# Two layers in one program: the second layer's first attentions beside the first layer's drain

## The reference

```python
x = x + tanh(g_xattn[0]) * L0_xattn(layernorm(x), ctx)   # 16 heads of 64, causal, key mask
x = x + tanh(g_ffn[0])   * L0_ffn(layernorm(x))          # attention between the 16 heads of a token,
                                                         # then 8 experts, summed by a softmax gate
x = x + tanh(g_xattn[1]) * L1_xattn(layernorm(x), ctx)   # 16 heads of 16, no mask
x = x + tanh(g_ffn[1])   * L1_ffn(layernorm(x))          # 2 experts of 256-1024-256 by top-1 of a token,
                                                         # and a shared one of the same size
```

## Time and profile before

| what | us |
|---|---|
| median of 3 runs | 2659.93 |
| the profiled execution | 2663.2 |
| its span | 2661.4 |
| one iteration of the first layer's loop | 78.4 |
| one iteration of the second layer's loop | 77.3 |
| first layer's two drain bodies | 65.0 and 32.0 |
| loads, splits and first projections of the second layer | 18.0 |
| second layer's body(0, None, 1) | 69.5 |

### The profile page before, as it was taken

How to read it: one execution, slowest core, us unless ns; L and a number is a source line. 1 busy time by engine, 2 the same in 40 slices (tenths; PEclk the granted TensorE clock), 3 DMA queues, 4 the chain that set the end, 5 groups by cost and what they waited for, 6 DMA issues and landing times. The chain is left out here.

```text
span 2661.4 us, 48220 instructions
## 1 busy us (share of the span) xinstructions
PE 2325.5 (87%) x16128; PEld 1931.7 (73%) x16128; DVE 1487.3 (56%) x3906; ACT 1268.0 (48%) x3971; POOL 1019.5 (38%) x910
## 2 busy tenths in 40 slices
PE   5888989888888898888466999999999999999998
PEld 4667777777777777776354777877777887777777
DVE  3467667666766676767635445444444544444441
ACT  5655566555556555556023444433344443334441
POOL 1355554555554455555512333222233322223320
PEclk9989999999999999999667999999999999999999
DMA  4000000000000000000040000000000000000000
GB/s 145 14 6 17 13 16 4 16 16 16 16 12 4 16 16 16 16 4 9 4 161 1 13 17 16 16 16 16 4 12 16 16 16 16 16 4 12 16 9 9
DMA packets 25856, 51.66 MB, mean 19 GB/s; under 512 B 6272, under 2 KB 7040, under 8 KB 24640
## 3 DMA queue, kind: packets, MB, share of 16 engines
q1 hardware_dynamic: 25792, 50.84, 5.7%
HBM read 42.44 MB, written 8.39 MB: 19 GB/s over the span
## 5 line engine op out<-in xcount | busy, mean ns | idle before, releaser
L1191 POOL TENSOR_SCALAR l_probs<-l_probs,l_rinv 128x256 f32<-128x256 f32 x512 | 238.4, 480 | 590.0 <-DVE l_rinv L1406 589.4
L1302 ACT ACTIVATE l_probs<-l_score,l_negmax 128x256 f32<-128x256 f32 x512 | 238.4, 472 | 265.0 <-DVE l_negmax L1401 265.0
L364 POOL TENSOR_TENSOR l_prod<-l_att,l_kv 128x2048 f32<-128x2048 f32 x64 | 287.4, 4527 | 180.7 <-DVE l_att L637 180.7
L350 POOL TENSOR_TENSOR l_prod<-l_q,l_kv 128x2048 f32<-128x2048 f32 x64 | 290.3, 4547 | 155.9 <-DVE l_att L620 84.1
L1606 PE MATMUL l_ffn<-l_w,l_hid 128*128 128x256 f32 x1536 | 347.9, 382 | 1.0 <-ACT l_hid L1276 1.0
L1606 PEld LDWEIGHTS l_ffn<-l_w,l_hid 128*128 128x128 f32 x1536 | 287.6, 190 | 51.0 <-issue 14.3
L1413 DVE COPY l_probsT<-l_attn 128x512 f32<-128x512 f32 x256 | 175.5, 685 | 161.1 <-PE l_attn L1569 160.9
L710 DVE CUSTOM_DVE_ANT_0 l_probs<-l_score,l_mbias 128x256 f32<-128x256 f32 (+1 forms) x512 | 161.3, 353 | 147.5 <-PE l_score L906 97.6
L1401 DVE TENSOR_REDUCE l_negmax<-l_score 128x2 f32<-128x512 f32 x256 | 175.1, 684 | 65.4 <-PE l_score L1557 65.4
L643 DVE TENSOR_REDUCE l_h<-l_prod 128x128 f32<-128x2048 f32 x64 | 146.3, 2286 | 110.7 <-POOL l_prod L364 110.7
L439 ACT ACTIVATE l_probs<-l_probs,l_negmax 128x256 f32<-128x256 f32 x256 | 130.8, 511 | 107.7 <-DVE l_negmax L710 106.5
(11 more groups left out here) (271 smaller groups left out, 7527.2 us busy)
## 6 DMA issues: line engine op xcount, KB each, us to landing
l_ctxin<-in_ctx SPq DMA_DIRECT2D x32, 256.0 KB, 3.0
l_xin<-in_x SPq DMA_DIRECT2D x16, 256.0 KB, 2.7
l_x<-in_x SPq DMA_DIRECT2D x16, 256.0 KB, 2.6
x<-l_acc SPq DMA_DIRECT2D x16, 256.0 KB, 2.0
l_xin<-x SPq DMA_DIRECT2D x16, 256.0 KB, 3.3
l_x<-x SPq DMA_DIRECT2D x16, 256.0 KB, 2.6
out<-l_x SPq DMA_DIRECT2D x16, 256.0 KB, 2.0
l_hid<-in_w SPq DMA_DIRECT2D x2, 1536.0 KB, 8.6
```

What stands on the lines that cost most here:

```text
L350: nc.gpsimd.tensor_tensor(prod[:, u].rearrange("p (h g d) -> p h g d", h=half, g=H), q4[:, u * half:(u + 1) * half].unsqueeze(2).to_broadc ...
L364: nc.gpsimd.tensor_tensor(prod[:, u].rearrange("p (h d g) -> p h d g", h=half, d=HD), a4.unsqueeze(2).to_broadcast([P, half, HD, H]), v4.u ...
L1191: last = nc.gpsimd.tensor_scalar(probs[:, j % 4, t * S:(t + 1) * S], probs[:, j % 4, t * S:(t + 1) * S], rinv[:, j, t:t + 1], 1.0, ALU.mul ...
L1302: last = nc.scalar.activation(probs[:, s % 4, t * S:(t + 1) * S], ps[:, t * S:(t + 1) * S], ACT.Exp, bias=negmax[:, s, t:t + 1], accum_out ...
```

## The change

`network` (new) builds both layers in one block. `layer0` and `layer1` no longer run a block; they return their five programs, now generators, and `side_by_side` interleaves the two programs of each engine by the position that each `yield` names. Both still have one order on each engine.

```diff
+BEGIN, BEGIN_OUT, TAIL = -0.8, -0.4, STEPS + 1
+FFN_LATE = STEPS - 6
+def side_by_side(*programs):
+    ahead = [(next(p), n, p) for n, p in enumerate(programs)]
+    while ahead:
+        _, n, p = ahead.pop(ahead.index(min(ahead)))
+        at = next(p, None)
+        if at is not None:
+            ahead.append((at, n, p))
```

Position 0 is step 0 of the first layer's last body with attention, `body(15, 14, 13)`; 21 (`TAIL`) is step 0 of the first drain body, 42 that of the second, whose steps are set half as far apart. The tail of every engine's program in layer0:

```diff
-                body(B - 1, B - 2, B - 3, None)
-                body(None, B - 1, B - 2, None)
-                body(None, None, B - 1, None)
+        for s in body(B - 1, B - 2, B - 3, None):
+            yield s
+        for s in body(None, B - 1, B - 2, None):
+            yield TAIL + s
+        for s in body(None, None, B - 1, None):
+            yield 2 * TAIL + s / 2
```

POOL's products of the mixing stand at 5.5, 6.5, 8.5, 9.5 and 13.5 to 16.5 of their body, the normalisation of head j of the second layer at j + 1. In layer1 the setup moves to the positions of body(15, 14, 13), body(0, None, 1) to those of the first drain body and body(1, 0, 2) to those of the second:

```diff
+    def sync(sp):
...
+        yield 6
+        _, full, _, turn = past.attn.at("q3", B - 1)
+        sp.wait_ge(full, turn)
+        load(0)
+        for n in range(NS_FIRST):
...
+        load(1)
+        yield TAIL + BEGIN
+        sp.wait_ge(past.x1_ready, B)
+        load_residual(0)
+        sp.dma_start(flat(wo), ins["wo1"]).then_inc(wo_in, 16)
+        for dst, src in late:
+            sp.dma_start(dst, src).then_inc(late_in, 16)
+        yield TAIL + STEPS
+        load(2)
+        yield 3 * TAIL
+        sp.wait_ge(past.x2_stored, 16 * B)
+        for n in range(NS_FIRST, NS):
+            sp.dma_start(raw(n), splits[n][0]).then_inc(raw_in[n % 2], 16)
+        sp.dma_start(flat(w2), ins["w2"]).then_inc(w2_in, 16)
+        load_residual(1)
+        store(0)
...
+    def scalar(act):
+        for n in range(NS_FIRST):
+            yield 9 + 2 * n
+            split(n)
+        yield TAIL + BEGIN
+        act.wait_ge(bias_ready, 1)
+        for use in attn.ahead:
+            project(use, 0)
+        for s in body(0, None, 1):
+            yield TAIL + s
+        for s in body(1, 0, 2):
+            yield 2 * TAIL + s
...
+    def vector(dve):
+        yield 9
+        pre_variance(0)
+        yield 11
+        split(0)
+        pre_normalise(0)
+        yield 13
+        split(1)
+        yield 15
+        split(2)
...
+        yield TAIL + BEGIN
+        dve.wait_ge(past.x1_ready, B)
+        for banks in (attn, score, heads):
+            banks.open(dve)
```

```diff
+    def up_at(b, s):
+        if first(b):
+            return range(12) if s == STEPS else ()
+        return (s,) if s < 12 else ()
```

On DVE, in step 12 and 13 of body(1, 0, None, 2), and on PE, behind the steps:

```diff
+                if first(b) and s == FFN_LATE - 2:
+                    dve.wait_ge(past.x2_ready, B)
+                    ffn.open(dve)
+                if first(b) and s == FFN_LATE - 1:
+                    for n in range(NS_FIRST, NS):
+                        split(n)
+                    begin(b)
...
+            if a is not None:
+                attn_out(a)
+            if b is not None:
+                if first(b):
+                    pe.wait_ge(split_lo, NS)
+                    for j in up_at(b, STEPS):
+                        ffn_up(b, j)
+                    pe.wait_ge(w2_in, 16)
+                    for piece in range(4):
+                        ffn_down(b, 0, piece)
+                for piece in range(4):
+                    ffn_down(b, 1, piece)
```

More of the change, by code:

```diff
@@ L8 @@
+from collections import namedtuple
 from contextlib import ExitStack
@@ L249, in layer0, with network @@
+def network(nc, ins, x2, out):
+    with ExitStack() as both:
+        with ExitStack() as left, ExitStack() as right:
+            one, past = layer0(nc, ins, x2, left, right, both)
+        with ExitStack() as left, ExitStack() as right:
+            two = layer1(nc, ins, x2, out, left, right, both, past)
         with nc.Block() as block:
@@ L289, in _ @@
-                load(2)
-                load_residual(1)
-                with sp.Fori(3, B) as b:
-                    load(b)
-                    load_residual(b - 1)
-                    store(b - 3)
-                load_residual(B - 1)
-                for b in (B - 3, B - 2, B - 1):
-                    store(b)
-                sp.wait_ge(x2_stored, 16 * B)
+                side_by_side(one.sync(sp), two.sync(sp))
             @block.gpsimd
             def _(pool):
-                nc.gpsimd.memset(ident[:], 0.0)
@@ L544, in _ @@
             def _(dve):
-                for banks in (attn, score, heads, side):
-                    banks.open(dve)
-                V = nc.vector
-                def variance(src, stat, mv, var, ready):
-                    for t in range(NT):
-                        V.bn_stats(stat[:, t], src[:, t])
-                    dve.drain()
-                    for t in range(NT):
-                        V.bn_aggr(mv[:, t], stat[:, t])
-                    dve.drain()
-                    V.tensor_scalar(var[:], mv[:, :, 1], LN_EPS, None, ALU.add).then_inc(ready, 1)
@@ L824, in _ @@
-                body(B - 1, B - 2, B - 3, None)
-                body(None, B - 1, B - 2, None)
-                body(None, None, B - 1, None)
+                side_by_side(one.vector(dve), two.vector(dve))
             @block.tensor
             def _(pe):
-                T = nc.tensor
-                def transpose4(banks, use, batch, src):
-                    ps, full, free, turn = banks.at(use, batch)
-                    pe.wait_ge(free, turn)
-                    for c in range(ND):
-                        for t in range(NT):
-                            last = T.transpose(ps[:, c * S + t * P:c * S + (t + 1) * P], src[:, t, c * P:(c + 1) * P], ident[:])
-                    last.then_inc(full, 1)
@@ L1683, in chunked @@
+                side_by_side(one.tensor(pe), two.tensor(pe))
 def chunked(w):
```

2626 lines of the change are left out of this document (1348 added, 1278 removed).

## The result

The changed kernel takes **2640.77 us** (median of 4 runs, 2637.36 to 2641.29), the kernel before beside it 2658.88: ratio 0.993, 95% interval 0.9913 to 0.9947. It is faster, and inside my range, but by 18 us where I had said 40. The profiled execution took 2640.78 us, its span 2639.0; the one of before took 2663.2, so the two profiles differ by 22.4 us, 4 more than the medians.

What follows compares the result with a forecast made beforehand. PE bounds the steady loop, but not the 269.1 us between the layers, forecast at 3.5 + 101 + 124.5 = 229. So 2663.2 - 40 = 2623, lowered by 3.3: 2620 us; own range 2608 to 2632, 8 in 10 2592 to 2648.

Steps and rivals of the forecast that it cites:

- (1): Second layer's setup moved under the first layer's last body: 3.5 us of delay there, 18 us between the layers gone.
- X: Mark where x1 of batch 15 is done, ending the first layer's last mixing body; forecast 3.5 us later, between 0 and 6.
- Wrong, if: Failure signs: A under 92 or over 112, w1 split waiting over 5 us for its transfer, later bodies not 77.3.
- (2): Second layer's attention of batch 0 beside the first layer's drain: 104 us, less 3 for the clock, 101.
- stage A: Stretch from x1 of batch 15 to x3 of batch 0, also called A: forecast 101 us.
- (3): Attention of batch 1 beside the experts of batch 15: 87.5 us, less 3 for the clock, 84.5; w1 about covered.
- (4): Feed forward of batch 0, alone on PE behind batch 1's attention: 40 us.
- stage B: Stretch from x3 of batch 0 to PE's third body of the second layer, also called B: forecast 124.5 us.
- Worse coupling: Rival, chance 0.15: POOL's normalisations behind products delay DVE's copies, each of eight products costing about 2 us; 2640 us.
- The clock stays at 1.2 GHz: Rival, chance 0.08: PE stays at the low clock, A 115 us with latencies, B 12 longer; 2646 us.
- Slower: Rival, chance 0.03: the layers' waits hold each other, nothing is covered, w1 adds 10.6 us in the open; 2669 us.

Runs made afterwards that it cites:

- e2: Changed kernel with DVE's whole second-layer setup moved to places where POOL runs no product, bias scaling behind x1 of batch 15: 2634.43 us.
- e1: Changed kernel with only the scaling of the second layer's query bias moved from step 15 to behind x1 of batch 15: 2634.11 us.
- e3: Kernel before plus one unused 128x2 SBUF-to-SBUF tensor_scalar on DVE at step 10 of each of 16 mixing bodies: 2725.72 us, ratio 1.0253.
- e8: Kernel before plus a 128x2 tensor_tensor add, all operands in SBUF, at step 10 of the 16 mixing bodies: 2726.52 us, ratio 1.0259.
- e4: Kernel before plus a 128x2 SBUF-to-SBUF reciprocal on DVE at step 10 of the 16 mixing bodies: 2660.0 us, ratio 1.0007.
- e5: e2, with the whole second layer's query taking its second input from PSUM, where ACT writes it in place: 2628.33 us, ratio 0.9891.
- e9: e6, with the last two of batch 15's reductions taken behind the copy of head 15: 2624.33 us, ratio 0.987.
- e11: e6 with the edits of both e9 and e10: 2628.47 us, ratio 0.988.
- e10: e6, with w1 split in steps 13 and 14 and eight of batch 0's twelve ups in steps 15 to 18: 2627.69 us.
- e7: Changed kernel with the second layer's attention begun only when the first layer is done: 2672.23 us, ratio 1.0047.
- e6: e5, with batch 0's feed-forward norm on DVE moved from the head of stage B to behind step 9: 2625.43 us, ratio 0.9881.
- e12: e8's add moved from step 10 to step 14 of the 16 mixing bodies: 2699.5 us (one run).

## Why the prediction was wrong, step by step

**The step that failed is (1), the setup under the last body: "what is put there delays all behind it: 1.8+1.2+0.7, less the small gaps, 3.5 us. The splits at 13 and 15 lie in gaps where DVE waits for POOL (...): nothing. X moves by +3.5, between 0 and 6."** It moved by 17.4. The work was counted nearly right: with the same work at quiet places (e2) X moved by 5.5. Wrong were the durations. I took 1.23, 1.22 and 0.69 us for the splits, not by scaling the 3.36 of the earlier trace rows, as I wrote (that gives 1.12 and 0.56), but as the trace of before has them from 1367.4 on, where POOL runs no product. I put them into gaps where DVE waits for POOL, that is, exactly where POOL is at work. (The 8.3 us of the earlier trace rows are those of the drain, too; ahead of the same four reductions in the last body itself they were 1.04, 2.10, 1.39 and 2.17 [before's timeline], 6.7 in all.) And the scaling of the bias, which isn't in my list at all, is one of the three long records. 12.1 us of waiting in three records, and with it an attn_out that grew from 7.14 to 10.08 us and came out into the open, are the 14 us missed (the split between the two is not exact, since part of the 12.1 fell into gaps); e1 and e2 took 7.7 and 11.9 of them back. Nothing of what I had named under "Wrong, if" came true, for it was all of A, w1 and the loop, and nothing in it watched X; the mark did, 1280.8 where I had said 1268.

The rule could have been read beforehand. The Trainium skill, SBUF — State Buffer, in "Who interferes with whom", says that a VectorE instruction with two SBUF inputs, or one such as tensor_scalar in a two-port mode, shares a port pair with GpSimd, that the pair is locked for a whole instruction, and that a reduction or an instruction with one SBUF input outside those modes doesn't contend. By that rule this case's traces agree: 4.04 us for the scalar and 4.03 for the add (e3, e8), 0.15 for the reciprocal (e4), and 0.75 for the query with an input in PSUM (e5). The first layer's own program had been a sign: beside its products DVE has reductions, reads of PSUM and reciprocals only.

**Step (2), stage A:** 101 forecast, 105.8 measured, 104.7 without the query's wait. Beginning and steps 0 to 13 took 75 us where I had 79 less 3 for the clock, and heads 0 and 7 stood at 13.0 and 44.7 us where I had 14 and 48: right. The tail took 31 instead of 25. POOL's chain of four products was 21.2, as forecast. But I let the tail end with the last reduction; it ends with attn_out, for which DVE waits 6.4 us more (1385.01 less the reduction's end). That is the term left out. Nearly half of it is the clock: the same 16 matmuls took 6.61 us here at 0.55 and 3.69 in stage B at 1.00.

```profile
1378.36 6.61 PE L1695 MATMUL l_attn<-l_wo,l_oT 128*128 128x256 f32 x16 [0.73 <-issue]
...
1466.66 3.69 PE L1695 MATMUL l_attn<-l_wo,l_oT 128*128 128x256 f32 x16 [0.73 <-issue]
```

The reduction ahead of the last head's copy isn't what holds attn_out: with e9's edit the copy came only 0.4 us sooner (93.4 behind X in e11, 93.8 in e6). What holds it shows in e11's rows: PE's last transposes wait for POOL's normalisation, which stands behind the third product, and DVE's copy waits for the transposes. A kernel with that normalisation elsewhere wasn't tried.

```profile
1363.47 0.63 PE L1676 MATMUL l_attn<-l_ident,l_probs 128*128 128x128 f32 x4 [1.82 <-POOL l_probs L1256]
1364.14 0.69 DVE L1497 COPY l_probsT<-l_attn 128x512 f32<-128x512 f32 x1 [1.84 <-PE l_attn L1676]
```

**Steps (3) and (4), stage B:** 124.5 forecast, 122.9 measured. The store came after 46.3 us, where I had x2 at 51, and w1 met step 13: DVE's wait for the first split is 2.79, ACT's cast alone. PE's feed forward begins at 1470.0, 83.5 us into B (forecast 84.5; my terms add up to 87.7 less 3, not 87.5 less 3), lasts 39.4 us (40), and is nearly without gaps at a clock of 1.00. Whether it stands wholly behind the attention or two thirds of its ups beside it makes no difference that can be measured (e10).

**The sum.** Between the marks of the two profiles, 36.5 of the forecast's 40 us are there in e5, where the long records are gone: +2.0 in X, +3.7 in A, -2.1 in B. The medians say less: e5 gains 29.2 us over the kernel before beside it. The rest is in the two executions profiled, of which before's was 3 to 6 us above its medians and e5's 2 below.

**The rivals.** "Worse coupling" gave 2640 and is the number that came, but not by its way: it had DVE's copies wait for POOL's normalisations in A, and A lost 5, while 14 were lost ahead of A; that the number fits is luck. "The clock stays at 1.2 GHz" is half there, since A had 0.79 on the mean and B's first part 0.78. "Slower", in which nothing is covered, is e7: 2672, where I had said 2669. That is in part luck too: I had 264 us for A and B together and 10.6 more for w1's transfer in the open, with 3.5 ahead of X; e7 has 258.6 for A and B with w1 in them, and 18.7 ahead of X.

The best measured kernels are e6 and e9, 2625.4 and 2624.3 us: 15 to 16 us less than the changed kernel and 32 to 35 less than before, from an order of DVE's setup, one operand in PSUM and a norm that waits.

## What to carry to other kernels

Before a DVE instruction is moved into a gap in which DVE waits for GpSimd, look at its operands: such a gap is no free place for an instruction with two inputs in SBUF, or a tensor_scalar between SBUF tiles, because it waits for GpSimd's running instruction, here 4 us for 128x2 values. Put such work where GpSimd waits for DVE (e2), or give it one operand in PSUM (e5). In the profile this wait is no idle time: it stands in the record's own duration, so compare one form's least, median and most.

## What the runs showed that I had not expected

- In the 8.40 us of the query (e1, e2) DVE let three ends of POOL instructions go by, while in the changed kernel, started equally long (2.04 us) after the same product began, it came at the first (3.07 us), and in e12 between two products 16 times of 16. What decides it stays open.
- POOL waits too: its product that began 0.17 us behind the start of a 0.68 us split took 4.87 us instead of 4.5, and two normalisations beside the query's 3.07 us record took 1.39 instead of 0.97.
- One more wait of 4 us in a body of 78 us was paid in full and more: 57.6 us of records cost 67.5 us (e3), though DVE idles 29% of a body.
- The same instructions of stage A took 39.0 or 43.6 us from X to the first reduction (e9, e11), with clocks of 0.89 and 0.67 in 20 us of that stretch. That is as much as two of my edits were meant to bring. That the clock is the cause isn't shown: e10, with the same instructions, had 0.76 there and took 43.5 us, no less than e11.
